# Decoder layer: the cross-attention's query projections by one level of Strassen's algorithm, scores earlier in each slot

## The reference

```
q = (hidden_states @ Wq.T).reshape(bsz, q_len, H, HD).transpose(0, 2, 1, 3)      # H = 32, HD = 128
k, v = the same of cross_attention_states with Wk, Wv     # KVH = 8
q = _rmsnorm(q, q_norm_w)
k = jnp.repeat(k, GROUPS, axis=1)            # each k and v head serves 4 query heads
v = jnp.repeat(v, GROUPS, axis=1)
k = _rmsnorm(k, k_norm_w)
scores = jnp.einsum('bhqd,bhkd->bhqk', q, k) * scale + mask
out = softmax(scores) @ v
return out.transpose(0, 2, 1, 3).reshape(bsz, q_len, H * HD) @ Wo.T
```

## Time and profile before

| | |
|---|---|
| three runs | 1006.45, 1006.81, 1007.21 us (median 1006.81) |
| the profiled execution | 1007.58 us |
| its span, first to last instruction | 1005.8 us |
| PE busy / DVE / ACT / POOL | 966.1 / 573.8 / 494.2 / 404.0 us |
| mean granted clock of PE | 0.986 of 2.4 GHz |
| chain that ended last, share of PE | 86% |

### The profile page before, as it was taken

How to read it: one execution, slowest core, us unless ns; L and a number is a source line. 1 busy time by engine, 2 the same in 40 slices (tenths; PEclk the granted TensorE clock), 3 DMA queues, 4 the chain that set the end, 5 groups by cost and what they waited for, 6 DMA issues and landing times.

```text
span 1005.8 us, 15353 instructions
## 1 busy us (share of the span) xinstructions
PE 966.1 (96%) x5010; PEld 804.8 (80%) x5010; DVE 573.8 (57%) x1340; ACT 494.2 (49%) x1368; POOL 404.0 (40%) x341
## 2 busy tenths in 40 slices
PE   5999799999999999899999999999999999999895
PEld 3866488878888888788888888888888888888782
DVE  3665554422321357566666666666566666666777
ACT  4655342422231246555654654654655555555554
POOL 4334634744443453342442442532622623514322
PEclk9999999999999999899999999999999999999997
DMA  6200013310111111011010020020020020100002
GB/s 218 82 3 31 12 46 125 105 63 0 63 63 63 44 62 56 22 43 43 22 54 29 21 83 0 21 83 0 21 83 0 27 78 0 63 0 0 1 1 85
DMA packets 12977, 45.60 MB, mean 45 GB/s; under 512 B 1617, under 2 KB 2257, under 8 KB 9873
## 3 DMA queue, kind: packets, MB, share of 16 engines
q1 hardware_dynamic: 12944, 45.20, 12.9%
HBM read 43.10 MB, written 2.10 MB: 45 GB/s over the span
## 4 chain that ended last, share of the span: by engine, by line
PE 86%; DVE 5%; POOL 3%; ACT 2%; issue 2%; DMA 1%; SPq 0%; POOLq 0%; DVEq 0%; ACTq 0%
PE bank L376 25%; PE bank L378 24%; PE bank L377 24%; PE bank L654 6%; PE bank L664 3%; PE bank L387 1%; POOL res L1438 1%; DVE cbuf L1638 1%; POOL rstd L1333 1%; PE bank L641 1%; DVE bst L1775 1%; POOL h_lo L1327 1%; DMA res<-in_x 1%; PE bank L455 1%; PE bank L744 0%
## 5 line engine op out<-in xcount | busy, mean ns | idle before, releaser
L376 PE MATMUL bank<-act_hi,w_hi 128*128 128x512 f32 x560 | 225.0, 402 | 2.0 <-DVE act_lo L1585 1.6
L378 PE MATMUL bank<-act_hi,w_lo 128*128 128x512 f32 x560 | 220.0, 393 | 0.0
L377 PE MATMUL bank<-act_lo,w_hi 128*128 128x512 f32 x560 | 220.0, 393 | 0.0
L1509 POOL TENSOR_TENSOR pb<-pb,prec 128x512 f32<-128x512 f32 x64 | 66.6, 1040 | 311.6 <-DVE prec L1910 311.6
L1161 ACT ACTIVATE pb<-pb,nmax 128x128 f32<-128x128 f32 x256 | 99.8, 391 | 79.1 <-DVE nmax L1905 79.1
L376 PEld LDWEIGHTS bank<-act_hi,w_hi 128*128 128x128 f32 x560 | 106.1, 189 | 25.6 <-issue 4.3
L378 PEld LDWEIGHTS bank<-act_hi,w_lo 128*128 128x128 f32 x560 | 106.1, 189 | 22.9
L377 PEld LDWEIGHTS bank<-act_lo,w_hi 128*128 128x128 f32 x560 | 106.2, 190 | 22.7 <-issue 1.4
L376 PE MATMUL bank<-w_hi,ot_hi 128*128 128x512 f32 x256 | 105.0, 410 | 0.8 <-DVE ot_lo L1585 0.8
L378 PE MATMUL bank<-w_hi,ot_lo 128*128 128x512 f32 x256 | 100.9, 394 | 0.0
L377 PE MATMUL bank<-w_lo,ot_hi 128*128 128x512 f32 x256 | 100.3, 392 | 0.0
(11 more groups left out here) (190 smaller groups left out, 2066.4 us busy)
## 6 DMA issues: line engine op xcount, KB each, us to landing
raw_a<-in_w_q SPq DMA_DIRECT2D x8, 1024.0 KB, 4.8
raw_b<-in_w_o SPq DMA_DIRECT2D x8, 1024.0 KB, 4.8
raw_a<-in_w_gu SPq DMA_DIRECT2D x7, 1024.0 KB, 5.3
raw_b<-in_w_kv SPq DMA_DIRECT2D x8, 512.0 KB, 3.3
raw_b<-in_w_dn SPq DMA_DIRECT2D x7, 512.0 KB, 3.3
res<-in_x SPq DMA_DIRECT2D x8, 256.0 KB, 6.1
raw_b<-in_ctx_t SPq DMA_DIRECT2D x8, 256.0 KB, 3.2
xre<-in_x SPq DMA_DIRECT2D x2, 1024.0 KB, 7.0
```

Source lines behind the costliest of these rows:

```text
L376: mm(o, l_hi, r_hi, start=first, stop=False)
L377: mm(o, l_hi, r_lo, start=False, stop=False)
L378: return mm(o, l_lo, r_hi, start=False, stop=last)
L1509: TT(pb[:, jj % 2, :, :], pb[:, jj % 2, :, :], prec[:, jj % 2, :].unsqueeze(2).to_broadcast([P, GH, L]), ALU.mult).then_inc(p_norm, 1)
```

## The change

Group 0 keeps its eight `q_step`s, three of them now in slot 0. For groups 1 to 7 the query projection is a product of 2 x 2 blocks: the weights' four blocks A11 to A22 (two heads by half of the 512 inputs) and the activations' four blocks B11 to B22 (half of the inputs by half of the tokens). By the variant of Strassen's algorithm with 7 products and 15 additions, PE does `q_prod(g+1, i)` for i = 0 to 6 in slots 1 to 7, each 2 banks x 2 mm3 = 12 matmuls of 512 columns. What else belongs to it:

- POOL makes the sums of weight blocks (`combine_s`, `combine_s1`, `combine_s4`: 4 subtractions or additions in each group) and some of the sums of products (`combine_u4`: 4). Each of the 7 combined blocks is split (`wp_hi` on ACT, `wp_rest` on POOL), where 4 were.
- The sums of activation blocks (T1 to T4) are made once: `combine_t3`, `combine_t1`, `combine_t2`, `combine_t4` are 20 operations of 128 x 512 on POOL in slots 0, 1 and 3 of group 0, then rounded on ACT (`t_round`) and DVE (`t_rest`).
- DVE adds the products 1 to 6 into `q_t` and two spare places (`q_add`, 2 operations each); ACT copies product 0 (`q_copy`). ACT no longer copies q out of the bank in the other slots; it squares it from `q_t` (`q_square`). `q2` has one buffer where it had two.
- `q_part` and its `q_square` stand where `PART_EARLY` (at the slot's start) and `PART_LATE` (at its end) say: as n = 1's heads 0 to 3 in slots 0 early, 1 early, 1 late, 2 early, and the next group's in 4 late, 5 early, 5 late, 6 early.
- The scores stand ahead of the query product in a slot with j < 3, and on ACT `softmax_exp` now stands before `pt_evac` there; in slots with j = 3 it stays behind it.
- The fold of the sums goes to columns 256 to 319 of bank 2, the transposed k to bank 7, and in slot 0 the second k and v product to bank 0.
- SP loads the query weights as four transfers of 256 KB and `w_o` as three.
- Slots 2 and 3 of group 0 have their query product behind `pv_step`.

```diff
-        WQ_SLOT = {1: (0, 1), 3: (2,), 4: (3,)}
+        WP_COL = [1024, 1536]
+        A11, A12, A21, A22 = 0, 1, 2, 3
+        BLOCK_AT = [A11, A11, A12, A21, A11, A12, A22]
+        PART_EARLY = {5: (1, 0, 3), 6: (1, 0, 1), 0: (0, 1, 0), 1: (0, 1, 1), 2: (0, 1, 3)}
+        PART_LATE = {4: (1, 0, 2), 5: (1, 0, 0), 1: (0, 1, 2)}
...
+            def q_prod(gn, i):
+                pe.wait_ge(wq_l, split_at(gn, i) + 1)
+                if isinstance(gn, int) and gn == 1 and i in (1, 2, 3, 6):
+                    pe.wait_ge(t_lo, {2: 2, 1: 4, 3: 6, 6: 8}[i])
+                if i == 0:
+                    pe.wait_ge(q_ev, 8 * gn)
+                    pe.wait_ge(kraw_done, 8 * gn - 2)
+                for m in range(2):
+                    if 1 <= i <= 3:
+                        pe.wait_ge(qc_done, 6 * gn - 6 + 2 * (i - 1) + m + 1)
+                    elif i > 3:
+                        pe.wait_ge(q_ev, 8 * gn + 2 * (i - 4) + m + 1)
+                    for k in range(2):
+                        c0 = WP_COL[i % 2] + (2 * m + k) * P
+                        b_hi, b_lo = prod_rhs(i, k)
+                        t = mm3(bank[m][:, :], w_hi[:, c0:c0 + P], w_lo[:, c0:c0 + P], b_hi, b_lo,
+                                k == 0, k == 1)
+                    t.then_inc(q_mm, 1)
...
-            def slot(g, jj, lead=True, before=True):
+            def slot(g, jj, make=True, before=True):
                 n, j = jj // HALF, jj % HALF
                 pg, pn = (g, 1) if n == 0 else (g + 1, 0)
+                behind = first_group(g) and jj in (2, 3)
+                turn = (g, jj + 1) if j < 3 else (pg, 4 * pn)
+                if j == 3:
+                    kt_step(pg, pn)
+                else:
+                    kv_step(pg, pn, j + 1 if j else 0)
+                    if before:
+                        s_step(*turn)
+                if make and jj and not behind:
+                    q_prod(g + 1, jj - 1)
+                if not before:
+                    q_step(1, 1)
                 if j == 0:
-                    kv_step(pg, pn, 0)
-                if j < 3:
-                    q_step(pg, pn, j + 1)
-                    kv_step(pg, pn, j + 1)
-                else:
-                    kt_step(pg, pn)
-                    if lead:
-                        q_step(g + 1, n, 0)
-                s_step(*((g, jj + 1) if j < 3 else (pg, 4 * pn)))
+                    kv_step(pg, pn, 1)
+                if not before:
+                    q_step(1, 2)
+                    q_step(1, 3)
+                if j == 3 or not before:
+                    s_step(*turn)
                 pt_step(g, jj)
                 if before:
                     d_step(*((g, jj - 1) if jj else (g - 1, 7)))
                 if j == 2:
                     qs_step(pg, pn)
                 pv_step(g, jj)
+                if make and behind:
+                    q_prod(g + 1, jj - 1)
...
+            def q_square(g, n, h):
+                i = head_at(g, n, h)
+                act.wait_ge(q_ev, i + 1)
+                if not (isinstance(i, int) and i == 0):
+                    act.wait_ge(qtr_done, i)
+                A(q2[:, :], q_t[:, n, h, :], ACT.Square).then_inc(qsq_done, 1)
...
-            def slot(g, jj, lead=True, refill=True):
+            def slot(g, jj, make=True):
                 n, j = jj // HALF, jj % HALF
                 pg, pn = (g, 1) if n == 0 else (g + 1, 0)
+                start = first_group(g)
+                turn = (g, jj + 1) if j < 3 else (pg, 4 * pn)
                 if j == 0:
                     kv_evac(pg, pn, 0)
-                if j < 3:
-                    q_evac(pg, pn, j + 1)
+                if jj in PART_EARLY and (make or jj < 3):
+                    d, qn, qh = PART_EARLY[jj]
+                    q_square(g + d, qn, qh)
+                if start and jj == 0:
+                    q_evac(1, 1)
+                if j == 3:
+                    kt_evac(pg, pn)
+                elif j:
                     kv_evac(pg, pn, j + 1)
-                else:
-                    kt_evac(pg, pn)
-                    if lead:
-                        q_evac(g + 1, n, 0)
+                if make and jj < 7 and jj != 1:
+                    wp_hi(g + 1, jj)
+                if j == 0:
+                    kv_evac(pg, pn, 1)
+                if start and jj == 0:
+                    q_evac(1, 2)
+                    q_evac(1, 3)
+                if j != 3 and not (start and jj == 0):
+                    softmax_exp(*turn)
                 pt_evac(g, jj)
-                softmax_exp(*((g, jj + 1) if j < 3 else (pg, 4 * pn)))
-                if refill and jj in WQ_SLOT:
-                    for h in WQ_SLOT[jj]:
-                        wq_hi(g + 1, h)
-                if jj == 0 and not (isinstance(g, int) and g == 0):
+                if j == 3 or start and jj == 0:
+                    softmax_exp(*turn)
+                if make and jj == 1:
+                    q_copy(g + 1)
+                    wp_hi(g + 1, jj)
+                if jj == 0 and not start:
...
+                if start and jj in (1, 2, 4):
+                    t_round(*{1: (t3, t3_raw, 6), 2: (t2, t2_raw, 16), 4: (t4, t4_raw, 20)}[jj])
                 ot_evac(g, jj)
+                if start and jj == 2:
+                    t_round(t1, t1_raw, 12)
+                if jj in PART_LATE and (make or jj < 3):
+                    d, qn, qh = PART_LATE[jj]
+                    q_square(g + d, qn, qh)
...
+            def combine_u4(gn):
+                pool.wait_ge(qc_done, 6 * gn)
+                for m in range(2):
+                    TT(q_t[:, 0, m, :], q_t[:, 0, m, :], u3_s[m], ALU.subtract).then_inc(s_cmb, 1)
+                pool.wait_ge(s_cmb, 8 * gn - 2)
+                for m in range(2):
+                    pool.wait_ge(q_ev, 8 * gn + m + 1)
+                    TT(q_t[:, 0, m, :], q_t[:, 0, m, :], q_t[:, 0, 2 + m, :], ALU.add).then_inc(s_cmb, 1)
...
-            def slot(g, jj, refill=True):
+            def slot(g, jj, make=True):
                 n, j = jj // HALF, jj % HALF
                 pg, pn = (g, 1) if n == 0 else (g + 1, 0)
                 if j == 2:
                     k_rsqrt(pg, pn)
+                if make and jj == 1:
+                    combine_s(g + 1)
+                if make and jj == 4:
+                    combine_s4(g + 1)
+                if make and jj < 7 and jj != 1:
+                    wp_rest(g + 1, jj)
+                if make and jj == 4:
+                    combine_u4(g + 1)
+                if first_group(g):
+                    if jj == 0:
+                        pool.wait_ge(q_mm, 4)
+                        pool.wait_ge(n_lo, 24)
+                        combine_t3()
+                        combine_t1()
+                    elif jj == 1:
+                        combine_t2()
+                    elif jj == 3:
+                        combine_t4()
                 p_scale(*((g, jj + 1) if j < 3 else (pg, 4 * pn)))
                 if j == 2:
                     q_rsqrt(pg, pn)
-                if refill and jj in WQ_SLOT:
-                    for h in WQ_SLOT[jj]:
-                        wq_rest(g + 1, h)
-                if jj == 0 and not (isinstance(g, int) and g == 0):
+                if make and jj == 1:
+                    wp_rest(g + 1, 1)
+                    combine_s1(g + 1)
+                if jj == 0 and not first_group(g):
...
+            def q_add(gn, i):
+                if i in (1, 5):
+                    dve.wait_ge(s_mm, 8 * gn - 4 if i == 1 else 8 * gn)
+                if i == 4:
+                    dve.wait_ge(s_cmb, 8 * gn)
+                for m in range(2):
+                    dve.wait_ge(q_mm, prod_at(gn, i) + m + 1)
+                    if i < 4:
+                        dve.wait_ge(qc_done, 6 * gn - 6 + 2 * (i - 1) + m + 1)
+                    o, first = ((q_t[:, 0, m, :], p1_s[m]), (u3_s[m], q_t[:, 0, m, :]),
+                                (q_t[:, 0, 2 + m, :], u3_s[m]), (q_t[:, 0, m, :], q_t[:, 0, m, :]),
+                                (q_t[:, 1, m, :], p1_s[m]), (q_t[:, 1, 2 + m, :], u3_s[m]))[i - 1]
+                    TT(o, first, bank[m][:, :], ALU.add).then_inc(qc_done if i < 3 else q_ev, 1)
...
-            def slot(g, jj, lead=True, before=True):
+            def slot(g, jj, make=True, before=True):
                 n, j = jj // HALF, jj % HALF
                 pg, pn = (g, 1) if n == 0 else (g + 1, 0)
                 turn = (g, jj + 1) if j < 3 else (pg, 4 * pn)
+                start = first_group(g)
                 if j == 0:
                     v_rest(pg, pn, 0)
                 if not before:
-                    q_part(0, 1, 0)
                     softmax_rec(0, 0)
+                if jj in PART_EARLY and (make or jj < 3):
+                    d, qn, qh = PART_EARLY[jj]
+                    q_part(g + d, qn, qh)
+                if j in (1, 2):
+                    v_rest(pg, pn, j + 1)
+                if j == 2:
```

(39 more changed lines are left out.)

407 lines of the change are left out of this document (286 added, 121 removed).

## The result

The changed kernel takes 1071.66 us (median of 4 runs, 1068.11 to 1073.43) against 1006.77 (1006.45 to 1007.21): ratio 1.064, 95% interval 1.0612 to 1.0667. The forecast was 1060, range 1034 to 1077, slower with 0.92. The profiled execution is at 1071.38, its span 1069.6, 63.8 more than before.

What follows compares the result with a forecast made beforehand. The prediction took PE, busy all 72.80 us of a loop group, as the bound. Loop groups +19.5, clock +4.9, group 0 +29 and tail 0 made +53.4 on the profiled 1007.58: 1061, by the median 1060 us, range 1034 to 1077.

Steps and rivals of the forecast that it cites:

- group in the loop, full clock: One loop group: 6.0 us of new waits for 2.75 us of matmuls saved, so 76.05 us, 3.25 longer.
- six groups, without the clock: Loop groups 1 to 6, each 3.25 us longer: +19.5 us.
- the clock behind slot 0: PE's clock drops after slot 0's wait, costing 1.64 us each time; half of six taken, +4.9 us.
- group 0 and what lies before it: Group 0's waits for activation sums and rests, clock losses and moved query tiles: +29 us, ends +18 and +35.
- tail: Group 7, slots 1 to 3 at the loop chain's length, a p_scale wait gone: about 0, ends -1.5 and +2.
- The chain from pv to pv: In-order ACT and DVE steps between pv starts outlast PE's work, in slot 2 10.20 against 9.16 us.
- 8.3 against 8.24: Loop slot 1: the chain's length against PE's own work in us, a wait of 0.06.
- the short waits: Loop waits of 1.1 us: under the 1.57 us idle that held the clock, so no clock loss.
- The second wait: Group 0, slot 1: PE waits 2.9 us for p_scale of item 2, behind POOL's sums.
- the one before product 1: Group 0, slot 2: product 1 waits 3.8 us for T2's rests on DVE, behind ot_lo.
- The saving: Rival: PE stays full and group 0's sums hide, so all 19.2 us are won: 987.6 us, chance 0.06.
- a clock that falls everywhere: Rival: slot 0's waits and also those of 1.1 us lower PE's clock: 1066 to 1076 us, chance 0.16.
- The rule of the Trainium skill: Two-SBUF-input DVE instructions contend with GpSimd SBUF reads under an exclusive lock; four rests charged 1.19 us each, not 0.68.

Runs made afterwards that it cites:

- e1_exp_back: The changed kernel with one step put back: on ACT pt_evac stands ahead of softmax_exp again in every slot; 1037.26 us, ratio 1.0318.
- e2_pt_ahead: The kernel of e1_exp_back with DVE's pt_rest right behind softmax_max, ahead of q_add and k_norm; 1025.75 us, ratio 1.0208.
- e7_short_late_part: The changed kernel with the transposition in the PART_LATE q_parts cut from 512 columns to 32; 1056.53 us, ratio 1.0497.
- e9_sums_and_tail: e2_pt_ahead plus group 0's sums reordered and shared by DVE and POOL, product 1's weights earlier, group 7's item 0 statistics off slot 2's chain; 1000.83 us.
- b1_exp_ahead: The kernel before the change, with only ACT's softmax_exp moved ahead of pt_evac in slots with j < 3; 1113.95 us, ratio 1.1073.

## Why the prediction was right in kind and 12 us short

By its own steps, in us on the profiled execution:

| step | forecast | measured |
|---|---|---|
| group in the loop, full clock | 76.05 | 77.08 |
| six groups, without the clock | +19.5 | +25.7 |
| the clock behind slot 0 | +4.9 | +4.8 |
| group 0 and what lies before it | +29 | +28.2 |
| tail | 0 | +4.8 |
| sum | +53.4 | +63.5, and 0.3 behind it |

So 6.2 of the 10.4 missing here are the loop's groups and 4.8 the tail (by the medians 11.7 are missing).

- *The chain from pv to pv.* The mechanism holds: e1_exp_back and e2_pt_ahead take it away step by step, at the sizes of its terms, and e7_short_late_part takes out one term alone. By slot the excess over PE's own work was, forecast and measured: slot 0 2.30, 2.24; 1 0.06, 0.11; 2 1.04, 1.47; 3 0, 0.15; 4 0.41, 0.33; 5 1.16, 1.35; 6 1.04, 1.20; 7 0, 0.13. The term that was mis-sized is slot 2's start: ot_hi was put 0.04 behind pv, and came 0.4 later, behind the rounding of product 1's weights. Slots 1, 3, 5, 6 and 7 add 0.1 to 0.2 each, slots 0 and 4 came out 0.1 shorter. In slots 5 and 6 a wait delays PE by 0.2 to 0.3 more than its idle time shows (10.36 for 0.98 idle in slot 6, which without a wait takes 9.09 in e9_sums_and_tail); slots 3 and 7 have no wait and are 8.10 and 8.08 in e9_sums_and_tail too, so there PE's own work was put 0.1 too low. (The prediction's "8.3 against 8.24" for slot 1 counts from the end of pv, the other slots from its start; the difference of 0.06 is the same.)
- *The clock.* Half of the slot-0 waits were to bring it down, at 1.64 each: it was four of the six that begin a loop group, at 78.29 - 77.08 = 1.21. The two errors cancel, which is luck. The reason given for the short waits, that under 1.57 idle nothing falls, does not hold in general: in b1_exp_ahead the clock fell behind 7 of 15 waits of 1.47 (last section).
- *Group 0.* From ACT's rounding of product 0's weights to the end of p_scale 18.4 was forecast; it took 19.05 (409.62 to 428.67), with 1.34 for a sum and not 1.29; PE's wait was 8.02 for 8.7. The second wait was 3.72 for 2.9, the one before product 1 2.66 for 3.8, that by T4's rests 1.2 (pv to pv of slot 5, 11.50 for 10.29) for 2.4. Together these are 15.6 for 17.8, and yet the whole is only 0.8 below its forecast. Part of the rest is a wait of 0.82 before the scores of slot 3 that was not counted, and the clock, granted 0.50 to 0.70 in the 5 us behind each of the three long waits; how it splits is not shown.
- *The tail* is the step whose mechanism failed. "About 0, ends -1.5 and +2" used the loop's chain for slots 1 to 3 of group 7. It is a different chain: DVE takes the statistics of item 0 between the two q_parts there, and the clock fell behind the wait. (Its 5.2 for slot 3 was not today's length either: the kernel before took 6.41 there, with 0.88 of wait before the scores.) DVE and PE in slot 2 of group 7 of the changed kernel:

```profile
994.19 0.68 DVE L2070 BATCH_NORM_STATS2 bst<-res 128x6 f32<-128x512 f32 x1
994.90 0.18 DVE L2072 BATCH_NORM_AGGREGATE mv<-bst 128x2 f32<-128x6 f32 x1
995.12 0.16 DVE L2074 TENSOR_SCALAR var<-mv 128x1 f32<-128x1 f32 x1
995.20 0.71 DVE L2159 STREAM_TRANSPOSE q2t<-q 128x512 f32<-128x512 f32 x1
```

```profile
1001.80 0.79 PE L474 MATMUL bank<-pt_hi,v_hi 128*128 128x512 f32 x1 [4.21 <-DVE pt_lo L1880]
...
1005.12 2.05 PE L783 MATMUL bank<-k_t,q_t 128*128 128x128 f32 x8 [0.83 <-issue]
```

  The statistics are 1.0 us, so slot 2 took 11.19 and not 10.2 (that they are in the chain shows in e9_sums_and_tail, where slot 2 fell by 0.8 without them); the next took 9.89 where it had taken 6.41, at the lower level of the clock (1.2 GHz: granted 0.50 from 1001.80 to 1010). Slot 4 gave 1.2 back, since its wait for p_scale fell from 1.57 to 0.33, as the forecast had it. With 0.4 in slot 1 that makes the 4.8.
- *The rivals.* The saving did not arrive; the chain was late in full. The measured 1071.7 lies in the band given for a clock that falls everywhere (1066 to 1076), but that is not its cause: it fell behind four of the six waits in slot 0, where the forecast had three, and in the loop never behind the waits of 1.0 to 1.2.
- *The rule of the Trainium skill.* I charged the rests of T2 and T4 at 1.19 because POOL would work beside them. For T3 it did (below), and they took 1.28 each; for T2 POOL stood in a power of 128x16, and they took 0.64, and for T4 POOL was idle, and they took 0.64 too. The first of these is why the wait before product 1 was 2.66 and not 3.8, 0.20 + 0.63 + 0.60 + 2 x 0.64 = 2.7.

## What to carry to other kernels

Work taken off the engine that is full pays only as far as the longest in-order chain through the other engines allows; sum that chain from one use to the next, by rows, and ask of each item whether the next user needs it now. Here nearly the same instructions in another order and on other engines were worth 71 us (1071.7 to 1000.8), and the best kernel is only 6 us below the one before, of the 19 that the arithmetic saved. And price the first and the last pass of a loop by their own instruction lists, since other work stands in their chains.
